# A state-space block and a two-of-eight expert layer on one core: small steps moved between engines, gated rows later in an expert, turned rows inside its second layer

## The reference

```
z  = layernorm(x)
u  = silu(causal_conv4(in_proj @ ctx) + conv_b)                  # 256 channels
B, C, dt_lo = x_proj @ u                                         # 16 states
delta = softplus(dt_proj @ dt_lo + dt_b)
state_t = state_(t-1) * exp(delta_t * A) + (delta_t * u_t) * B_t # per channel and state
y  = (sum_n state * C + D * u) * silu(z)
x1 = x + y
probs = softmax(layernorm(x1) @ Wg); the two best of 8 experts per token
each expert takes at most 320 tokens, in token order; the others are dropped
out = x1 + sum over the chosen experts of prob * (relu(row @ w1[e]) @ w2[e])
```

## Time and profile before

| what | value |
|---|---|
| runs | 292.21, 292.71, 296.63 us; median 292.71 |
| profiled execution | 291.2 us, its span 289.2 us |
| busy share | PE 85%, PEld 77%, DVE 77%, ACT 61%, POOL 77% |
| instructions in the span | 5031 |
| mean granted TensorE clock | 0.913 of full speed |
| HBM | 143 GB/s over the span |

### The profile page before, as it was taken

One profiled execution on the slowest core, in us unless ns is written; L12 is line 12 of the kernel. 1 busy time (PEld: TensorE's weight loads), 2 busy tenths in 40 slices (PEclk: granted clock), 3 DMA queues, 4 the chain that ended last, 5 costly groups with the idle time before them and its releaser, 6 DMA issues.

```text
span 289.2 us, 5031 instructions
## 1 busy us (share of the span) xinstructions
PE 245.1 (85%) x1564; PEld 222.3 (77%) x1564; DVE 223.8 (77%) x372; ACT 175.5 (61%) x384; POOL 222.1 (77%) x177
## 2 busy tenths in 40 slices
PE   8968787495959388698699997999999999999990
PEld 7746475374747277577689987999999999999980
DVE  2789999799999999999978845859485757575710
ACT  1888856938996776639528354475655647374500
POOL 1599769878996999998743828988787878787761
PEclk9998979979968955559999999999999999999995
DMA  6669540053001905025032575455464655645110
GB/s 158 231 189 332 191 170 0 0 187 145 0 1 34 333 0 185 0 57 199 21 117 39 211 233 202 153 169 202 156 201 183 191 213 178 226 179 180 38 59 23
DMA packets 15073, 40.38 MB, mean 140 GB/s; under 512 B 2922, under 2 KB 9900, under 8 KB 12112
## 3 DMA queue, kind: packets, MB, share of 16 engines
q1 hardware_dynamic: 11792, 33.15, 33.9%
q0 software_dynamic: 2816, 6.32, 6.4%
q10 hardware_dynamic: 448, 0.70, 0.9%
HBM read 32.72 MB, written 8.49 MB: 143 GB/s over the span
## 4 chain that ended last, share of the span: by engine, by line
PE 38%; POOL 23%; issue 16%; DVE 9%; DMA 8%; ACT 3%; POOLq 1%; ACTq 1%; SPq 0%; DVEq 0%
PE ps L1057 10%; PE ps L1059 9%; PE ps L1058 9%; POOL dbu L359 7%; DVE hc L1295 3%; DVE h L1276 3%; POOL expert_rows L404 2%; DMA cwb<-in_conv_w 2%; DMA expert_rows<-xrow,sloti 2%; POOL w1raw L366 2%; PE ps L862 2%; DMA xe<-expert_rows 2%; PE ps L1066 2%; DVE h L1283 2%; POOL delta L377 1%
## 5 line engine op out<-in xcount | busy, mean ns | idle before, releaser
L359 POOL TENSOR_TENSOR dbu<-du,bsb 128x1024 f32<-128x1024 f32 x31 | 72.6, 2358 | 0.4
L572 ACT ACTIVATE ps<-delta,anegs 128x255 f32<-128x255 f32 x128 | 53.0, 462 | 12.3 <-DVE h L1276 9.1
L1478 DVE SCALAR_TENSOR_TENSOR htlo<-ps,hthi 128x320 fp32r<-128x320 f32 x64 | 30.7, 488 | 31.8 <-ACT hthi L740 31.8
L473 POOL DMA_INDIRECT so_far<-out,dst x24 | 34.3, 1429 | 13.7 <-DVE dst L1466 6.9
L840 PE MATMUL ps<-stack,sels 64*128 64x256 f32 x64 | 17.5, 360 | 31.2 <-DVE hc L1295 28.2
L862 PE MATMUL ps<-cst,hc 128*128 128x128 f32 x256 | 42.2, 318 | 1.4 <-DVE hc L1295 1.4
L1276 DVE TENSOR_TENSOR_SCAN h<-ps,dbu 128x1024 f32<-128x1024 f32 x18 | 41.1, 2282 | 0.1
L840 PEld LDWEIGHTS ps<-stack,sels 64*128 64x128 f32 x64 | 11.0, 215 | 39.2 <-issue 38.8
L463 POOL TENSOR_TENSOR w2lo<-w2raw,w2hi 128x512 fp32r<-128x512 f32 x28 | 36.3, 1321 | 6.1 <-ACT w2hi L632 5.9
L1057 PE MATMUL ps<-xthi,w1hi 128*128 (+1 forms) x124 | 39.3, 317 | 1.9 <-DVE htlo L1478 1.6
L740 ACT ACTIVATE hthi<-ps 128x320 fp32r<-128x320 f32 x64 | 28.0, 438 | 20.0 <-PE ps L1059 20.0
(11 more groups left out here) (183 smaller groups left out, 528.8 us busy)
## 6 DMA issues: line engine op xcount, KB each, us to landing
w1raw<-in_w SPq DMA_DIRECT2D x8, 1024.0 KB, 5.2
w2raw<-in_w SPq DMA_DIRECT2D x8, 1024.0 KB, 4.9
bsb<-b_rows SPq DMA_DIRECT2D x7, 1024.0 KB, 7.2
expert_rows<-fill SPq DMA_DIRECT2D x1, 2580.0 KB, 15.8
xe<-expert_rows SPq DMA_DIRECT2D x8, 258.0 KB
out<-x SPq DMA_DIRECT2D x4, 256.0 KB, 5.2
xnat<-in_x SPq DMA_DIRECT2D x1, 768.0 KB, 7.3
xe<-expert_rows SPq DMA_DIRECT2D x8, 64.5 KB
```

Of the source, the lines that this page charges most:

```text
L359: nc.gpsimd.tensor_tensor(dbu[j % DRING][:], du[:, :, None, cols(b)].to_broadcast([P, EC, 2, L]), bsb[b % 2][:, None, 2 * p:2 * p + 2, :]. ...
L473: nc.gpsimd.indirect_dma_start(so_far[0:EROWS[t], t, :], None, out, bass.IndirectOffsetOnAxis(ap=dst[0:EROWS[t], e * ET + t, :], axis=0), ...
L572: ins = nc.scalar.activation(decays(g % SLOTS_DA)[:, c, i * L + 1:(i + 1) * L], delta[:, c, b * L + 1:(b + 1) * L], ACT.Exp, scale=anegs[: ...
L1478: nc.vector.scalar_tensor_tensor(out=htlo[:, f, :], in0=ps[:, f % 4, 0:CAP], scalar=0.0, in1=hthi[:, f, :].bitcast(F32), op0=ALU.max, op1= ...
```

## The change

1. GpSimd: the destinations of all eight tiles are written by one copy with a broadcast operand, not by eight.
2. GpSimd: `z_rstd(2, ...)` is issued before `delta_u(1)`, no longer after the next `drive`.
3. Last sequence: `nrx`, `ntop` and the gates are made by GpSimd, not by ScalarE.
4. VectorE: `gated_rows(e - 1)` follows hidden tile f = 4, not f = 1.
5. TensorE: `turn_rows(e + 1)` and its wait for the gated rows stand after the first tile of layer 2, not between the layers.
6. VectorE: the first convolution takes its taps in another order, and the first tap of each half waits for that half's product alone; in expert 0 the row numbers of expert 0 (`metas(0, True)`) are taken before `rows_lo(1)`.

```
@@ gpsimd
-            for j in range(TILES):
-                ins = nc.gpsimd.tensor_copy(xrow[:, j, :, DM + 1], cst[:, CDST + j:CDST + j + 1].to_broadcast([P, TOPK]))
-            ins.then_inc(s["const_done"], 1)
+            nc.gpsimd.tensor_copy(xrow[:, :, :, DM + 1], cst[:, CDST:CDST + TILES, None].to_broadcast([P, TILES, TOPK])
+                                  ).then_inc(s["const_done"], 1)
...
                         softplus_delta(b + 1)
+                        if b == 0:
+                            z_rstd(2, slice(BT, TILES))
                         delta_u(b + 1)
-                if b == 0 and p == 5:
-                    z_rstd(2, slice(BT, TILES))
...
+            nc.gpsimd.tensor_scalar(nrx[:, tiles_of(B - 1)], rx[:, tiles_of(B - 1)], -1.0, None, ALU.mult
+                                    ).then_inc(s["ln_neg"], 1)
+            pool.wait_ge(s["ln_neg"], B)
+            pool.wait_ge(s["oh_done"], B)
+            nc.gpsimd.tensor_tensor(ntop[:, tiles_of(B - 1)], top[:, tiles_of(B - 1), 0], nrx[:, tiles_of(B - 1)], ALU.mult
+                                    ).then_inc(s["top_bias"], 1)
             pool.wait_ge(s["xe_in"], 32)
+            pool.wait_ge(s["weights_sum"], B)
+            for j in tiles_range(B - 1):
+                ins = nc.gpsimd.tensor_scalar(xrow[:, j, :, DM], etop[:, j, 0:TOPK], rsum[:, j:j + 1], None, ALU.mult)
+            ins.then_inc(s["gates_done"], 1)
             pool.wait_ge(s["gates_done"], B)
@@ scalar
             def top_exp(b):
-                act.wait_ge(s["oh_done"], b + 1)
-                for j in range(b * BT, (b + 1) * BT):
-                    ins = nc.scalar.activation(ntop[:, j:j + 1], top[:, j, 0:1], ACT.Copy, scale=nrx[:, j:j + 1])
-                ins.then_inc(s["top_bias"], 1)
+                if b < B - 1:
+                ...
                 act.wait_ge(s["top_bias"], b + 1)
...
-            nc.scalar.activation(nrx[:, tiles_of(B - 1)], rx[:, tiles_of(B - 1)], ACT.Copy, scale=-1.0
-                                 ).then_inc(s["ln_neg"], 1)
-            act.wait_ge(s["ln_neg"], B)
             top_exp(B - 1)
...
-            weigh(B - 1)
@@ tensor
-                if not last and not first:
-
-                    pe.wait_ge(s["r_done"], ET * e)
-                    turn_rows(e + 1)
...
                     for f in range(FC):
+                        if not last and not first and f == 1:
+                            pe.wait_ge(s["r_done"], ET * e)
+                            turn_rows(e + 1)
@@ vector
-            dve.wait_ge(s["xe0_psum"], EC)
-            for k, c, steps in ((0, 0, 0), (0, 1, 0), (1, 0, 1), (2, 0, 3), (1, 1, 2), (3, 0, 4), (2, 1, 5), (3, 1, 6)):
+            for k, c, steps in ((0, 0, 0), (1, 0, 1), (0, 1, 0), (2, 0, 2), (1, 1, 3), (3, 0, 4), (2, 1, 5), (3, 1, 6)):
+                if k == 0:
+                    dve.wait_ge(s["xe0_psum"], c + 1)
...
-                    if f == 1 and not first:
+                    if f == 4 and not first:
                         gated_rows(e - 1)
...
                     metas(e + 1, False)
-                    rows_lo(e + 1)
                     if first:
                         metas(0, True)
+                    rows_lo(e + 1)
```

More of the change, by code:

```diff
@@ L600, in top_exp @@
             def top_exp(b):
-                act.wait_ge(s["oh_done"], b + 1)
-                for j in range(b * BT, (b + 1) * BT):
-                    ins = nc.scalar.activation(ntop[:, j:j + 1], top[:, j, 0:1], ACT.Copy, scale=nrx[:, j:j + 1])
-                ins.then_inc(s["top_bias"], 1)
+                if b < B - 1:
+                    act.wait_ge(s["oh_done"], b + 1)
+                    for j in range(b * BT, (b + 1) * BT):
+                        ins = nc.scalar.activation(ntop[:, j:j + 1], top[:, j, 0:1], ACT.Copy, scale=nrx[:, j:j + 1])
+                    ins.then_inc(s["top_bias"], 1)
                 act.wait_ge(s["top_bias"], b + 1)
```

## The result

The changed kernel takes 297.71 us (median of 4 runs, 295.71 to 298.33); the kernel before took 292.86 beside it (292.21 to 296.63). The profiled execution took 297.38 us (span 295.6, before 289.2). The profiled executions lie 6.2 us apart and not 4.85, since the one before, at 291.2, was 1.7 under its median.

What follows compares the result with a forecast made beforehand. TensorE bounds the middle experts at 15.4 us each; the loop through GpSimd's sends and w2's load would replace it. −0.5 − 0.2 − 0.6 + 11.75 + 3.3 = +13.8 us on 291.2, put at 305.5; range 296 to 310.

Steps and rivals of the forecast that it cites:

- The meeting: GpSimd's w2 splits meet VectorE's w1 splits, each half waits for one split: +1.2 us per expert; bounds 0 and 2.5.
- the loop: Sends, second w2 split, next w2 load, ScalarE's roundings, gated row: 16.55 us without the meeting, 17.75 with, against TensorE's 15.4.
- expert 1: TensorE's 1.61 us wait goes (−1.7 with restart); a wait for w2 at layer 2's fifth tile adds 1.1: net −0.6.
- the end: Expert 7 and after: expert 6's results sent 3.5 us later, less 0.25 the last scatter waits for TensorE: +3.3.
- Rival B: The loop without the meeting: 16.55 us a turn, +6.8 us in all, 298.0 to 299.5 us; chance 0.23.
- A: The loop with the meeting of splits: 305.5 us; chance 0.57.
- the direct way: Layer 2's fifth tile waits for w2's third quarter, split behind the sends; priced in expert 1: 0.5 us, 1.1 with the meeting.
- z's scale: Put before du: a new 1.3 us wait for dbu replaces a 1.74 us wait: −0.5; bounds +1.3 and −1.7.
- The copy of destinations: Front: frees up to 0.9 us, VectorE's 0.65 wait goes, decays are met earlier: 0; bounds 0 and −0.65.
- The convolution's order: Front: hidden behind TensorE's twelve padding products, which end at 9.35: 0; bounds 0 and −0.3.
- Gates on GpSimd: Last sequence: gates move from behind ScalarE's rounding of rows to idle GpSimd: −0.2 us; bounds −0.4 and +0.5.
- Turned rows inside layer 2: TensorE: moves a set of products past a tile and adds none: 0.

Runs made afterwards that it cites:

- e7: Changed kernel with VectorE's w1 splits from the second expert on cut to 8 of 256 columns: 296.48 us, ratio 1.015.
- e8: Changed kernel with each w2 load made in two halves, the first waiting only for the quarters split ahead of the sends: 296.61 us, ratio 1.013.
- e11: Kernel before with only gated rows at the fifth hidden tile and rows turned inside layer 2: 299.86 us, ratio 1.025.
- e1: Changed kernel with gated rows after the second hidden tile again: 288.42 us, ratio 0.984.
- e4: Kernel before with only the copies, z's scale, gates on GpSimd, convolution's order and expert 0's row numbers: 288.27 us, ratio 0.986.
- e2: Changed kernel with gated rows after the third hidden tile: 289.49 us, ratio 0.989.
- e5: Changed kernel with gated rows after the fourth hidden tile: 291.46 us, ratio 0.994.
- e6: Changed kernel with gated rows after the sixth hidden tile: 302.43 us, ratio 1.031.
- e3: Changed kernel with all four quarters of w2 split on GpSimd ahead of the sends: 296.68 us, ratio 1.015.
- e9: Changed kernel with w2's last two quarters split by VectorE behind the sixth and seventh hidden tiles: 296.31 us, ratio 1.017.
- e10: e9 with GpSimd making those two splits again behind the sends, into an unread tile, and w2's load waiting for them: 310.12 us, ratio 1.061.

## Why the prediction was wrong

**The step that failed** is the one term "GpSimd's two halves each wait for one w1 split: +1.2". The meeting takes place, and within the 0.2 us that I gave it (w1's splits at 263.10, w2's second half at 263.19). But I took 1.2 as the turn-taking of the earlier trace rows, and misread them. GpSimd's two splits lost 0.4 there (2.99 for 2.58), a third of my term. VectorE's two lost 1.6: they took 2.92, and two by themselves

```profile
170.35 1.28 DVE L1392 TENSOR_TENSOR w1lo<-w1raw,w1hi 128x512 fp32r<-128x512 f32 x2
```

So my own rows showed that VectorE pays the most, and I laid all of it on GpSimd. In the meeting of this loop GpSimd's two splits, one behind the other, lose nothing and VectorE waits until both are through. e7 shows that the loop is as long when VectorE's side of the meeting is next to nothing. I had said that 0 was the bound if they missed each other; it is also the value if they meet and the other engine waits. That is 5 × 1.2 = 6.0 of the middle's 11.75, 0.6 of expert 1 and 0.4 of the end. Rival B, which differs in just this term, gave +6.8 and 298.0 to 299.5; measured are +6.4 in the span and 297.71 as the median. I had it at 0.23, with A at 0.57. By A's signs sends should have come 17 to 18 us apart, and some w2 and w1 splits taken 1.2 to 2 us; sends came 16.2 to 17.3 apart, no w2 split of GpSimd took over 1.32, and a w1 split took up to 3.35.

**The loop**, forecast at 16.55 without that term, is 16.37: load to rounding 5.0 for 5.0, ScalarE to gated row 4.42 for 4.55, wake and scatters 4.41 for 4.4, splits 2.53 for 2.6. The first send comes 6.0 us behind the turn of results where it came 3.3 behind, 2.75 later for the 2.6 that I had. Experts 2 to 6 cost +5.5 for the 5.75 that it gives. In it, expert 2 had a slower landing of w2: 5.8 us, outside the 4.7 to 5.2 of the earlier trace rows, with ScalarE's wait at 1.72:

```profile
189.05 0.63 ACT L642 ACTIVATE w2hi<-w2raw 128x512 fp32r<-128x512 f32 x1 [1.72 <-DMA w2raw<-in_w]
...
DMA to landing us min/median/max: 4.7/4.9/5.8
```

**What I had not seen** is that the direct way is nearly as long. For expert 1 I worked out that TensorE waits 0.5 for the third quarter (measured 0.57, at 182.19), and did not carry it to the others, where e8 shows it by itself at 16.19. It changed no number here, since the loop covers it. It would have spoiled any repair of the load alone.

**Expert 1**: −0.6 forecast, −1.2 without the meeting, −1.05 measured. TensorE's wait in layer 1 is gone; fetches begin at 168.25 for 171.30. **The end**: +3.3 forecast, +3.1 measured. The first scatter of expert 6 takes 0.8 longer there, beside VectorE's w2 split. The prediction had no such term, so that the end came out so near is in part luck:

```profile
275.81 1.86 POOL L491 DMA_INDIRECT out<-eo,dst  x1 [1.92 <-DVE eo L1495]
...
282.18 1.05 POOL L482 DMA_INDIRECT so_far<-out,dst  x1 [1.98 <-DMA out<-eo,dst]
...
289.11 0.92 POOL L491 DMA_INDIRECT out<-eo,dst  x1 [0.30 <-issue]
```

**z's scale**: −0.5 forecast. From the scan at 28.50 to that at 53.41 were 24.91 us; now 24.34, so −0.57. The new wait is where it was forecast and the old one is gone:

```profile
48.99 2.34 DVE L1289 TENSOR_TENSOR_SCAN h<-ps,dbu 128x512 f32<-128x512 f32 x2 [1.11 <-POOL dbu L358]
...
52.35 2.33 DVE L1289 TENSOR_TENSOR_SCAN h<-ps,dbu 128x512 f32<-128x512 f32 x2
```

**The copy of destinations**, 0 forecast: it takes 0.21 us, the wait of 0.65 at 20.82 is gone, and VectorE meets ScalarE's decays earlier instead, as said:

```profile
28.01 2.34 DVE L1289 TENSOR_TENSOR_SCAN h<-ps,dbu 128x512 f32<-128x512 f32 x2 [0.72 <-ACT ps L581]
```

**The convolution's order**, 0 forecast: open within the start's scatter. The first scan begins at 16.46 and not at 17.38. In the other kernels with the new order it began at 16.24 to 17.48, and in e11, with the old one, at 18.79. The spread among kernels with one and the same start is over 1 us, so the 0.9 can't be given to the change. **Gates on GpSimd**, −0.2 forecast: at the scan at 52.35 the changed kernel is 1.06 us ahead of the one before (53.41), at the first turned results 1.15. So the gates and all else in between gave 0.1. **Turned rows inside layer 2**, 0 forecast: e1 beside e4 shows 0.

**What is open.** The end does not grow evenly with the place of the gated rows (16.03, 18.47, 18.26, 19.14, 19.62). The landing of expert 6's scatters took 3.6 us in e2 and 2.8 in e5 for 2.0 in the others, and a scatter was 0.3 longer in e2, 0.8 in the changed kernel, 0.4 in e6. Taken off, that leaves 16.0, 16.5, 17.5, 18.3 and 19.2, near one tile for each place. Why the landings varied was not tested; e2's profiled execution took 292.62 us, 3 over its median. Nor was out's loop taken away together with the two others.

## What to carry to other kernels

Before an operation is put later, write down every way from it back to the busiest engine: when two are within a few tenths, mending one brings nothing (e8), and the mended one can open a third (e3, e9). When two engines must meet at a shared resource, ask which of them waits and whether it has the time, before the loss is put on the critical one. And the work between a scatter and a dependent fetch is cover for the landing: taken out of there, it comes back as idle time on the queue.

The faster versions are the simplest: all parts of the change with the gated rows left at the second tile (e1, 0.984 of the time before), or the small parts alone (e4, 0.986).

## What the runs showed of the hardware

- In the changed kernel and in e7 two w2 splits of GpSimd one behind the other hold VectorE's two-input split for their whole length, even one of 16 elements a partition (up to 2745 ns for 164), and lose nothing themselves (1282 to 1321 ns). That is no rule for every meeting. Before the change, in expert 0, GpSimd's pair lost 0.4 us and VectorE's 1.6, and in e10, where VectorE's split had started 0.4 to 0.7 us earlier, GpSimd's pair took 3.02 to 3.04 for 2.69. What decides between these was not tested.
- With GpSimd's indirect DMAs it can be the other way round. A scatter or fetch takes 0.92 to 1.05 us beside nothing. Beside one two-input split of VectorE's some took 1.86, beside four 2.7 to 3.06, while VectorE's splits kept their length (2.48 for four in e10). e1, with w1's splits beside its fetches:

```profile
243.76 2.72 POOL L482 DMA_INDIRECT so_far<-out,dst  x1 [0.30 <-issue]
```

  Others were not held. In e3 a scatter lay wholly within four such splits and took 0.96; what decides was not tested:

```profile
229.81 0.96 POOL L491 DMA_INDIRECT out<-eo,dst  x1 [0.30 <-issue]
```

```profile
229.29 2.49 DVE L1398 TENSOR_TENSOR w1lo<-w1raw,w1hi 128x512 fp32r<-128x512 f32 x4
```

- GpSimd's wait for scatters to have landed in out was 2.0 us at the shortest and 5.43 at the longest. The three of 5.0 to 5.4, all in e9, had w2's 1 MB load and the loads of the next rows issued among the scatters. But 3.6 (e2) came with no such load near.
